# Two graph layers on one core: row sums scaled in PSUM, moments moved behind the output, one addition moved from GpSimd to ScalarE, loops written out

## The reference

```
# layer 0
h  = relu(layernorm(x))                          # over the 512 features
A  = adj @ h                                     # both of the layer's matrices are adj, so C - A = b
x1 = x + relu(max over columns of A + b)         # one number per row (node)
# layer 1
h  = relu(layernorm(x1))
q, k, v = h @ Wq + bq, h @ Wk + bk, h @ Wv + bv
w  = softmax(q k^T / 8 + (-1e9 where adj == 0))  # for each of 8 heads
out = x1 + w @ v
```

## Time and profile before

| | |
|---|---|
| median of 3 runs | 1386.8 us |
| the profiled execution's own time | 1386.83 us |
| its span, first to last instruction | 1384.9 us |
| PE busy | 1304.8 us, 94% |
| PE weight loads busy | 676.4 us, 49% |
| DVE busy | 1066.9 us, 77% |
| ACT busy | 879.7 us, 64% |
| POOL busy | 1242.3 us, 90% |
| DMA queue of the data (q1) | 55.3% of 16 engines |
| granted TensorE clock, mean | 0.98 |

### The profile page before, as it was taken

How to read it: one execution, slowest core, us unless ns; L and a number is a source line. 1 busy time by engine, 2 the same in 40 slices (tenths; PEclk the granted TensorE clock), 3 DMA queues, 4 the chain that set the end, 5 groups by cost and what they waited for, 6 DMA issues and landing times.

```text
span 1384.9 us, 32665 instructions
## 1 busy us (share of the span) xinstructions
PE 1304.8 (94%) x11145; PEld 676.4 (49%) x11145; DVE 1066.9 (77%) x2228; ACT 879.7 (64%) x1294; POOL 1242.3 (90%) x1288
## 2 busy tenths in 40 slices
PE   4899999999999999999999999999999999999982
PEld 1344545545455555545545455454545555455542
DVE  6458787787887887887887877878877878878777
ACT  4566666666666676666666666666766666666552
POOL 2888999999999999999999999999999999999852
PEclk8999999999999999999999999999999999999995
DMA  7244555555555565555555555555555555555445
GB/s 199 62 81 111 137 127 124 129 127 129 123 129 136 115 130 129 127 122 136 129 118 132 124 129 126 129 132 118 129 131 123 130 131 125 118 136 122 97 81 129
DMA packets 441378, 171.71 MB, mean 124 GB/s; under 512 B 406784, under 2 KB 406912, under 8 KB 441344
## 3 DMA queue, kind: packets, MB, share of 16 engines
q1 hardware_dynamic: 440000, 171.03, 55.3%
q10 hardware_dynamic: 1344, 0.27, 0.1%
HBM read 37.03 MB, written 33.55 MB: 51 GB/s over the span
## 4 chain that ended last, share of the span: by engine, by line
PE 75%; DVE 18%; issue 4%; DMA 1%; SPq 0%; DVEq 0%; POOL 0%; ACT 0%; POOLq 0%; ACTq 0%
PE proj L631 38%; PE proj L643 19%; PE sc L660 7%; PE o_ps L675 7%; PE proj L616 4%; DVE y L474 4%; DVE masked L451 3%; DVE row_max L455 3%; DVE out_scale L467 2%; DVE a_max L435 1%; DVE stats L417 1%; DVE v L440 1%; DVE inv_sum L465 1%; DMA x_in<-in_x 0%; DVE shifted L458 0%
## 5 line engine op out<-in xcount | busy, mean ns | idle before, releaser
L631 PE MATMUL proj<-hT,w 128*128 128x512 f16 x3072 | 689.8, 381 | 11.3 <-DMA hT<-h 6.8
L631 PEld LDWEIGHTS proj<-hT,w 128*128 128x128 f16 x3072 | 291.2, 98 | 361.0 <-issue 17.5
L643 PE MATMUL proj<-w,hT 128*128 128x512 f16 x1536 | 352.4, 379 | 1.1 <-DVE w L526 1.1
L451 DVE SCALAR_TENSOR_TENSOR masked<-sc,score_scale,mask 128x1024 f32<-128x1024 f32 x125 | 160.4, 1283 | 241.2 <-PE sc L660 241.2
L289 POOL TENSOR_TENSOR qkT<-qk,qkT 128x512 f16<-128x512 f32 x256 | 296.5, 1158 | 9.4 <-ACT qk L347 9.2
L296 POOL TENSOR_TENSOR probs<-probs 128x1024 f16<-128x1024 f32 x128 | 273.3, 2135 | 25.2 <-ACT probs L364 25.2
L345 ACT ACTIVATE qkT<-proj,bqk_up 128x512 f16<-128x512 f32 x256 | 173.4, 677 | 170.7 <-PE proj L631 170.7
L277 POOL TENSOR_TENSOR xbv<-x_in,bv_rows 128x512 f32<-128x512 f32 x128 | 276.2, 2158 | 0.0
L643 PEld LDWEIGHTS proj<-w,hT 128*128 128x128 f16 x1536 | 150.0, 98 | 182.8 <-DVE w L526 1.5
L474 DVE SCALAR_TENSOR_TENSOR y<-o_ps,out_scale,x 128x64 f32<-128x64 f32 x1024 | 208.2, 276 | 11.2
L458 DVE TENSOR_TENSOR shifted<-masked,row_max 128x1024 f32<-128x1024 f32 x128 | 189.2, 1478 | 4.4
(11 more groups left out here) (59 smaller groups left out, 937.6 us busy)
## 6 DMA issues: line engine op xcount, KB each, us to landing
x_in<-in_x SPq DMA_DIRECT2D x128, 256.0 KB, 2.6
out_x<-y SPq DMA_DIRECT2D x128, 256.0 KB, 2.3
hT<-h SPq DMA_TRANSPOSE x128, 3.1
probsT<-probs SPq DMA_TRANSPOSE x128, 4.3
w_raw<-in_L_gnn_Wq SPq DMA_DIRECT2D x1, 1024.0 KB, 9.2
w_raw<-in_L_gnn_Wv SPq DMA_DIRECT2D x1, 1024.0 KB, 11.4
w_raw<-in_L_gnn_Wk SPq DMA_DIRECT2D x1, 1024.0 KB, 13.4
bv_rows<-in_L_gnn_bv ACTq DMA_DIRECT2D x1, 256.0 KB, 6.8
```

Of the source, the lines that this page charges most:

```text
L451: nc.vector.scalar_tensor_tensor(masked[:, :, :], banks[:, :, :].rearrange("p t (h n) -> p (t h) n", n=P), score_scale[:, :], mask8[:, :]. ...
L631: last = nc.tensor.matmul(proj[:, u % 2, :], w16[:, j, s, c, col * P:(col + 1) * P], hT[:, k // GROUP % 2, t, c, :, :].rearrange("p g n -> ...
L643: last = nc.tensor.matmul(proj[:, V_BANK, :], hT[:, k // GROUP % 2, s, c, k % GROUP, :], w16[:, 2, t, c, :], start=(c == 0 and i == 0), st ...
```

## The change

Five things, all in how the same result is worked out:

1. The sums of the probabilities are first multiplied by a scale as they are read from PSUM (`scaled_sum`, a `tensor_scalar`), and the reciprocal of that, from SBUF, is the scale of the output. Before, the reciprocal came first, from PSUM, and the multiplication second, from SBUF. For that `redo` gets a third column, worked out once in the head.
2. On DVE, `stats_of` and `moments_wait` stand behind `attention_out` instead of ahead of it.
3. ACT adds the row constant: `xc = x_in + c_col` (an activation with a bias, last in ACT's slot, two buffers). POOL adds `bv` to that, one instruction in place of two, last in POOL's slot instead of first.
4. As `x_in` is now read last by ACT, the load of x waits for `xc_done`, and x is loaded 7 slots ahead instead of 8.
5. `slots` has no hardware loop: PE, ACT, DVE and POOL have all 128 slots written out, with constants in the waits.

```diff
-LOAD_AHEAD, MOMENTS_AHEAD, NORM_AHEAD, TURN_AHEAD, PREP_AHEAD, AMAX_AHEAD = 8, 6, 5, 5, 4, 3
+LOAD_AHEAD, MOMENTS_AHEAD, NORM_AHEAD, TURN_AHEAD, PREP_AHEAD, AMAX_AHEAD = 7, 6, 5, 5, 4, 3
...
         def slots(eng, slot, after_first=None):
 
-            for k in range(RING):
+            for k in range(B):
                 slot(0, k)
                 if k == 0 and after_first:
                     after_first()
-            with eng.Fori(RING, B - 2 * RING + 1, RING) as base:
-                for k in range(RING):
-                    slot(base, k)
-            for k in range(RING):
-                slot(B - RING, k)
...
-                    wait(sp, x1_done, base + k - RING + 1)
+                    wait(sp, xc_done, base + k - RING + 1)
                     sp.dma_start(x_in[:, k % RING, :], x[base + k, :, :]).then_inc(x_loaded[k % RING], 16)
...
-            def add_c(base, k):
+            def add_bv(base, k):
 
                 if in_range(base, k):
                     m = base + k
                     wait(pool, y_done, m - RING + 1)
-                    wait(pool, x1_done, m)
-                    pool.tensor_tensor(xbv[:, :], x_in[:, k % RING, :], bv_rows[:, :], ALU.add).then_inc(xc_done, 1)
                     pool.wait_ge(xc_done, m + 1)
-                    pool.wait_ge(c_done, m + 1)
-                    pool.tensor_tensor(x1[:, k % RING, :], xbv[:, :],
-                                       c_col[:, k % RING, :].to_broadcast([P, D]), ALU.add).then_inc(x1_done, 1)
+                    pool.tensor_tensor(x1[:, k % RING, :], xc[:, k % 2, :], bv_rows[:, :], ALU.add).then_inc(x1_done, 1)
...
-                add_c(base, k)
                 rest(base, k + NORM_AHEAD)
                 qk_rest(base, k, u)
                 norm_scales(base, k + MOMENTS_AHEAD)
                 probs_rest(base, k - ATTN_BEHIND)
                 qk_rest(base, k, u + 1)
+                add_bv(base, k)
...
                     act.wait_ge(a_evac, m + 1)
-                    wait(act, x1_done, m - RING + 1)
                     nc.scalar.activation(c_col[:, k % RING, :], a_max[:, k % RING, :], ACT.Relu, scale=down[:, 3:4],
                                          bias=b0_col[:, :]).then_inc(c_done, 1)
+
+            def add_c(base, k):
+
+                if in_range(base, k):
+                    m = base + k
+                    act.wait_ge(c_done, m + 1)
+                    wait(act, x1_done, m - 1)
+                    nc.scalar.activation(xc[:, k % 2, :], x_in[:, k % RING, :], ACT.Identity, bias=c_col[:, k % RING, :]).then_inc(xc_done, 1)
...
                 exps(base, k - ATTN_BEHIND)
                 qk_out(base, k, u + 1)
+                add_c(base, k)
...
                     dve.wait_ge(o_ready, m + 1)
-                    nc.vector.reciprocal(inv_sum[:, :, :], o_view[:, :, :, HD]).then_inc(inv_sum_done, 1)
-                    dve.wait_ge(inv_sum_done, m + 1)
-                    nc.vector.tensor_scalar(out_scale[:, :, :], inv_sum[:, :, :], undo[:, 2:3], None,
-                                            ALU.mult).then_inc(out_scale_done, 1)
+                    nc.vector.tensor_scalar(scaled_sum[:, :, :], o_view[:, :, :, HD], redo[:, 2:3], None,
+                                            ALU.mult).then_inc(sum_done, 1)
+                    dve.wait_ge(sum_done, m + 1)
+                    nc.vector.reciprocal(out_scale[:, :, :], scaled_sum[:, :, :]).then_inc(out_scale_done, 1)
                     dve.wait_ge(out_scale_done, m + 1)
...
                 nc.vector.tensor_scalar(undo[:, j:j + 1], down[:, j:j + 1], 1.0 / P_SCALE, None, ALU.mult).then_inc(undo_done, 1)
+                dve.wait_ge(scale_done, i + 1)
+                nc.vector.tensor_scalar(redo[:, j:j + 1], up[:, j:j + 1], H_SCALE * P_SCALE, None, ALU.mult).then_inc(redo_done, 1)
                 if j < 2:
-                    dve.wait_ge(scale_done, i + 1)
-                    nc.vector.tensor_scalar(redo[:, j:j + 1], up[:, j:j + 1], H_SCALE * P_SCALE, None, ALU.mult).then_inc(redo_done, 1)
-                    dve.wait_ge(redo_done, j + 1)
+                    dve.wait_ge(redo_done, i)
...
                 v_rest(base, k - V_BEHIND)
+                attention_out(base, k - Y_BEHIND)
                 stats_of(base, k + MOMENTS_AHEAD)
                 moments_wait(base, k + MOMENTS_AHEAD)
-                attention_out(base, k - Y_BEHIND)
                 moments_of(base, k + MOMENTS_AHEAD)
```

More of the change, by code:

```diff
@@ L63, in graph_layers @@
         undo = sb("undo", [P, 3])
-        redo = sb("redo", [P, 2])
+        redo = sb("redo", [P, 3])
         score_scale = sb("score_scale", [P, 1])
@@ L74, in graph_layers @@
         x_in = sb("x_in", [P, RING, D])
-        xbv = sb("xbv", [P, D])
+        xc = sb("xc", [P, 2, D])
         x1 = sb("x1", [P, RING, D])
@@ L97, in graph_layers @@
         probsT = sb("probsT", [P, 2, 2, H, P], F16)
-        inv_sum = sb("inv_sum", [P, 2, H // 2])
+        scaled_sum = sb("scaled_sum", [P, 2, H // 2])
         out_scale = sb("out_scale", [P, 2, H // 2])
@@ L130, in graph_layers @@
         probsT_done = [sem(f"probsT_done{i}") for i in range(2)]
-        o_ready, inv_sum_done, out_scale_done, y_done = sem("o_ready"), sem("inv_sum_done"), sem("out_scale_done"), sem("y_done")
+        o_ready, sum_done, out_scale_done, y_done = sem("o_ready"), sem("sum_done"), sem("out_scale_done"), sem("y_done")
         c_done, xc_done, x1_done = sem("c_done"), sem("xc_done"), sem("x1_done")
@@ L580, in _ @@
             dve.wait_ge(undo_done, 3)
+            dve.wait_ge(redo_done, 3)
             def k_rest():
```

## The result

| | before | after | forecast |
|---|---|---|---|
| median | 1386.7 us (4 runs) | 1374.5 us (4 runs, 1374.12 to 1375.62) | 1354.5, range 1352.5 to 1364 |
| ratio to before | 1 | 0.9912 [0.9895, 0.9929] | 0.977 |
| span of the profiled execution | 1384.9 us | 1372.6 us | 1352.6 |
| `masked` of slot 8 to that of slot 120 | 1155.85 us | 1141.9 us | 1123.6 |

The kernel is faster, by 12.2 us (0.9%, clear of the noise) where 32.3 were forecast. The time is above the range. Of the span's 12.3 us, 14.0 come from the steady part; 1.3 are given back in the head (slot 8 has its `masked` at 110.23 us, before at 108.98) and the rest behind slot 120.

What follows compares the result with a forecast made beforehand. PE was taken as the bound, at 10.03 us a slot, with late slots from DVE stalls. Reaching that floor over 112 slots gives back 32.3 us, other terms 0: 1386.83 - 32.3 = 1354.5 us, range 1352.5 to 1364.

Steps and rivals of the forecast that it cites:

- The floor: PE's steady slots without waits: 10.03 us each, so 1123.6 us from slot 8 to slot 120.
- The loop registers make the stall: Register instructions put 0.2 us before `inv_sum`, so `out_scale` meets POOL; writing out should give most of 32.3 us.
- Fetching costs nothing: Instruction fetches for the written-out programs on PE, ACT, DVE and POOL: taken as 0 us.
- rival (c): Written-out instructions come late: at most 91 more packets, 100 us if waited for in full, 1455 us; chance 0.02.
- The pair from PSUM 0.44 us: DVE's scaled sum from PSUM and reciprocal from SBUF together take 0.44 us, as the old pair did.
- rival (b): The reciprocal from SBUF inherits the stall at 1.16 us, making `y` late: 1399 us; chance 0.03.
- Moments behind the output cost nothing for POOL: `stats` behind `y` on DVE: `mean_var` starts at 8.0 us as before, cost 0; slack of `y` grows 0.1 to 0.8.
- ScalarE's addition is hidden: ACT's added activation, 0.81 us a slot, fits where ACT idles 1.19 us for PE before v's evacuation.
- The head at 0: One more scale instruction of about 0.15 us lies where DVE waits for ACT in the head: 0 us.
- rival (a): POOL's addition holds up DVE's `shifted`, `y` 0.25 us late; every third slot 9 us, 1364 us; chance 0.22.

Runs made afterwards that it cites:

- e1: The kernel after with `a_max` and the rest of v moved ahead of `masked` in DVE's slot: 1354.0 us, ratio to before 0.9767.
- e5: The kernel after with a POOL memset of an unread 128 x 384 tile just ahead of the addition of bv: 1355.1 us, ratio to before 0.9773.
- e4: The kernel before with only the slot loop written out: 1360.0 us, ratio to before 0.9803.
- e9: The kernel after with `stats` and the moments' wait ahead of the output again: 1395.6 us, ratio to before 1.0062.
- e3: The kernel after with POOL doing both additions first in its slot again and x loaded 8 slots ahead: 1360.2 us, ratio to before 0.9803.

## Why the prediction was wrong

- **The floor**: right. e1 and e5 take 1123.5 us from slot 8 to 120; forecast 1123.6.
- **The loop registers make the stall**: right, shown by e4 and by the chain beside it. Their share was "most of the 32.3 us": 26.7.
- **Fetching costs nothing, rival (c)**: right. 88 packets in all, 72 more than before (at most 91 more were counted), and e1 is at the floor with all its slots written out.
- **The pair from PSUM 0.44 us, rival (b)**: right, 0.21 and 0.20, the longest 0.23 and 0.20; nothing held up in any run.
- **Moments behind the output cost nothing for POOL**: right. `mean_var` comes at the same time in either order (the 1.19 of the formula holds in e9), and `y` has its slack. What the slack is worth was not forecast: in the kernel as changed 21 us (e9), without edits 3 and 4 nothing that e3 shows.
- **ScalarE's addition is hidden**: right in the steady part, at 0.72 us and not 0.81.
- **The head at 0**: wrong, 1.3 us. The step counted one more scale instruction; it did not ask what POOL, freed of its additions at the start of slot 0, would meet on DVE. The rests of Wk took 4.66 us instead of 2.74, and `a_max` behind them was late.
- **The step that failed** is what `shifted` costs when it meets the addition. The forecast's sum has nothing for it, and rival (a), which is what happened, prices it too low. "They meet, and hold each other up" came true, and so did "in every third slot", which was a case chosen for a price and not worked out, so that its fit is luck. The price was "`y` ends at 7.4 + 1.0 = 8.4, 0.25 us late", hence 9 us and 1364. But `y` is not the first thing behind `shifted` for which PE waits. That is `a_max`, with 0.32 us of slack instead of 0.8; a late slot costs 0.49 us, and 37 of them 18. With that price case (a) would have been 1354.5 + 18.3 = 1372.8, and with the head's 1.3 the time measured, to 0.4 us.
- **Its chance, 0.22,** was too low, and that could have been worked out: `mean_var` was put at 8.0 us after `masked`, with a `shifted` of 1.44 us. In 4.6 us more POOL is at the addition (in the kernel before it takes 4.5 from `var_eps` to L277, 634.90 to 639.43): 8.0 + 0.17 + 4.6 - 10.03 = 2.74 after the next `masked`. `shifted`, with less of POOL's work in front of it there, comes down from 1.44 to its 1.22 within two slots, and the addition with it, to 2.52: ahead of the 2.57 at which `shifted` starts. The forecast's own numbers had the collision in them. "A late `shifted` makes POOL late too and so works against it" was right and does not prevent it; it only sets how often.

## What to carry to other kernels

When an instruction can be held up, give the stall its price at every consumer behind it, in order, beginning with the next instruction on its engine: the slack of the last one says nothing of the first. When an edit makes a saturated engine wait for another, work out the start of its instructions anew, slot after slot, from the event that now releases it; if each quiet slot brings two rivals for one resource closer, they will meet. An instruction whose result is wanted soon belongs ahead of one that can be stalled, above all if its engine has idle time there.

## What the runs showed of the hardware

- Where DVE and POOL each have a `tensor_tensor` with its inputs in SBUF, the second stands until the first is nearly done, even if it starts only 0.02 us behind it (`shifted` 2.33 us instead of 1.22, beside an addition of 1.27). It works both ways: POOL's addition takes 1.27 us when it is first and 2.1 to 2.3 when it is second.
- A POOL write of 128x384 took 0.42 us and held up nothing. A `reciprocal` of 8 columns from SBUF took 0.20 us in all kernels that have it, where a `tensor_scalar` of the same size took up to 1.16.
- The loop's 112 slots as straight code on four engines cost nothing that the traces show: 88 packets of instructions, 0.4% of the DMA engines' time, and e1 runs at the floor.
- Register instructions for the counts of waits put 0.2 us ahead of a DVE instruction in two slots of eight, and to take the loop away was worth 26.7 us in this kernel.
